# A three-block transformer kernel on eight cores: one weight pass over four PSUM banks in the expert layers, routing weights applied after the down projection, and full-width value matmuls

## What is computed

```python
def ffn(x, ...):                          # called twice
    x = x + mla(rmsnorm(x, w_ln1), ...)
    return x + moe(rmsnorm(x, w_ln2), ...)

def mla(xn, ...):                         # 16 heads of 64
    ...
    scores = einsum('bqhd,bkhd->bhqk', qq, kk) / 8      # causal
    probs = softmax(scores)
    y = einsum('bhqk,bkhd->bqhd', probs, v)
    return y @ W_o

def moe(xn, ...):                         # 7 routed experts, 2 per token
    shared = silu(xt @ Wg_s) * (xt @ Wu_s) @ Wd_s
    probs = sigmoid(xt @ W_router + routing_bias)
    scores, idx = top_k(probs, 2)
    wts = one_hot(idx, 7) weighted by scores / sum(scores)
    hmid = silu(xt @ Wg_r[e]) * (xt @ Wu_r[e])          # every e
    combined = sum_e wts[:, e] * (hmid[e] @ Wd_r[e])
    return shared + combined
```

## Time and profile before

| what | value |
|---|---|
| median of 2 runs | 8025.83 us |
| the two runs | 8085.91 and 7965.74 us |
| profiled execution, its time | 7965.88 us |
| its span, slowest core (core 7) | 7964.3 us |
| spans of the 8 cores | 7933.8 to 7964.3 us |
| mean granted clock of TensorE, by core | 0.780 to 0.786 of full speed |

### The profile page before, as it was taken

The page is one execution under the profiler, slowest core; times in us unless marked ns, Lnnn a source line. Parts: engine busy times, 40 slices in busy tenths (PEclk is TensorE's granted clock), DMA queues, the critical chain, the costliest instruction groups (busy, mean ns, idle before and its releaser), DMA issues.

```text
span 7964.3 us, 84976 instructions; the slowest of 8 cores (7933.8 to 7964.3 us)
## 1 busy us (share of the span) xinstructions
PE 5230.4 (66%) x21368; PEld 2042.4 (26%) x21368; DVE 2696.5 (34%) x5979; ACT 1441.0 (18%) x2520; POOL 110.8 (1%) x147
## 2 busy tenths in 40 slices
PE   2556544665642749999994853565662559999996
PEld 0222211111111314444442321111111223444442
DVE  2333335224223323333333354324223333333332
ACT  1222210442430101111111010342440001111110
POOL 0000000000000000000000000000000000000000
PEclk9556567777776879999997966677776779999998
DMA  5000132001014322222224123001003431221113
GB/s 118 6 6 14 17 83 52 8 11 22 11 25 96 78 43 32 32 33 32 32 32 96 21 42 88 10 11 22 11 8 68 102 64 22 39 36 32 32 32 85
DMA packets 390961, 319.60 MB, mean 40 GB/s; under 512 B 277889, under 2 KB 292737, under 8 KB 390530
## 3 DMA queue, kind: packets, MB, share of 16 engines
q0 software_dynamic: 73584, 145.83, 11.3%
q1 hardware_dynamic: 316946, 168.34, 8.7%
HBM read 287.70 MB, written 79.82 MB: 46 GB/s over the span
## 4 chain that ended last, share of the span: by engine, by line
PE 58%; DVE 12%; issue 9%; ACT 8%; DMA 7%; SPq 3%; DVEq 2%; ACTq 0%; POOL 0%; POOLq 0%
PE PS L210 57%; ACT SCF L220 6%; DVE SCF L215 3%; DVE SCB L215 3%; SPq L78 3%; DVE SM L215 2%; DVE XNT L215 2%; DMA d_xn<-SCF 1%; ACT SCA L220 1%; DMA SCB<-d_yraw 1%; DVE SCA L215 1%; DVEq L73 1%; PE PS L1169 1%; DMA d_lo<-SCB 1%; DVE STAT L215 1%
## 5 line engine op out<-in xcount | busy, mean ns | idle before, releaser
L210 PE MATMUL PS<-XNT,WB 128*128 128x512 bf16 x9472 | 2078.6, 383 | 560.7 <-DVE XNT L215 433.2
L210 PEld LDWEIGHTS PS<-XNT,WB 128*128 128x128 bf16 x9472 | 932.5, 99 | 1701.5 <-issue 605.1
L210 PE MATMUL PS<-WB,SCA 128*128 128x512 bf16 x4864 | 1094.1, 388 | 316.7 <-DMA SCA<-d_y 271.6
L220 ACT ACTIVATE SCF<-PS,SM 128x512 bf16<-128x512 f32 (+3 forms) x1280 | 771.0, 622 | 1093.1 <-PE PS L210 966.9
L210 PE MATMUL PS<-SCF,SCA 128*65 128x512 bf16 x1280 | 615.8, 481 | 421.1 <-DVE SCF L215 205.5
L220 ACT ACTIVATE SCA<-PS 128x512 bf16<-128x512 f32 x640 | 374.8, 595 | 2430.9 <-PE PS L210 2206.4
L210 PEld LDWEIGHTS PS<-WB,SCA 128*128 128x128 bf16 x4864 | 480.3, 100 | 920.6 <-issue 378.4
L215 DVE TENSOR_TENSOR R<-PS,R 128x512 f32<-128x512 f32 x640 | 442.7, 692 | 806.7 <-PE PS L210 806.7
L210 PE MATMUL PS<-XNT,SCA 128*128 128x512 bf16 x1280 | 614.4, 494 | 12.0 <-DVE SM L215 9.5
L215 DVE TENSOR_TENSOR SCF<-SCF,CONSTB 128x128 bf16<-128x128 bf16 x512 | 105.9, 207 | 964.9 <-ACT SCF L220 960.7
L210 PEld LDWEIGHTS PS<-SCF,SCA 128*65 128x65 bf16 x1280 | 150.6, 118 | 883.7 <-issue 860.2
(11 more groups left out here) (122 smaller groups left out, 2658.3 us busy)
## 6 DMA issues: line engine op xcount, KB each, us to landing
WB<-wg_r POOLq DMA_DIRECT2D x28, 1024.0 KB, 12.4
WB<-wu_r POOLq DMA_DIRECT2D x28, 1024.0 KB, 22.3
WB<-wd_r POOLq DMA_DIRECT2D x28, 1024.0 KB, 11.2
d_xn<-SCF SPq DMA_DIRECT2D x96, 256.0 KB, 2.1
sp_x<-R SPq DMA_DIRECT2D x8, 2048.0 KB, 17.3
R<-sp_x POOLq DMA_DIRECT2D x8, 2048.0 KB, 27.6
R<-x SPq DMA_DIRECT2D x4, 2048.0 KB
SCA<-XNT SPq DMA_DIRECT2D x32, 256.0 KB, 3.3
```

What stands on the lines that cost most here:

```text
L210: return e.matmul(out_ap, lhsT, rhs, start=start, stop=stop, tile_position=tp)
L220: return getattr(e, name)(*a, **kw)
```

## The change

Four things are done.

1. The value matmul of the causal attention takes 128 stationary columns from the same start, where it took 65, and writes all 128 rows of bank 5. Rows 65 on are not read. A memset clears the end of SCA once at the start.
2. Gate and up of a hidden tile `ic` take all 8 banks: banks 0 to 3 are gate for the four token blocks, banks 4 to 7 up. The loop over `c` is outside, the one over token blocks inside, so that 4 matmuls in a row have the same stationary operand.
3. The eviction follows in the same `ic`: silu of a gate bank (which then is free), then one VectorE multiply of the silu scratch with the up bank. `wts_prep` with its transposes, matmuls and copies is gone.
4. The down projection has `ic` outside and the two halves inside, and both banks are added behind the 16 matmuls. For a routed expert the addition is a `scalar_tensor_tensor` that multiplies by the token's weight from `WTS`, which is a column of one number per partition there.

```diff
+    v_op("memset", SCA[:, 16704:17408], 0.0)
...
-                            mm(PS[5][0:65, :],
-                               SCA[:, vcol(pkc) + 65 * hl:vcol(pkc) + 65 * hl + 65],
+                            mm(PS[5][:, :],
+                               SCA[:, vcol(pkc) + 65 * hl:vcol(pkc) + 65 * hl + 128],
                                SCF[:, 512 * pslot:512 * pslot + 512],
...
-                def wts_prep(ee):
...
-                wts_prep(0)
...
             for ic in range(ND):
-                for lh in range(2):
-                    t = 2 * ic + lh
-                    bks = (0, 1, 2, 3) if t % 2 == 0 else (4, 5, 6, 7)
...
+                for c in range(ND):
+                    for lb in range(4):
+                        bk = lb
+                        w0 = (p.use(f"ps{bk}") + [(s_tp, v_xnt), (s_dv, v_gain),
+                                                  (s_wl[0], vl_g)]
+                              if c == 0 else ())
+                        mm(PS[bk][:, :],
+                           WB0[:, c * D + 128 * ic: c * D + 128 * ic + 128],
+                           XNT[:, c * S + 512 * lb: c * S + 512 * lb + 512],
+                           start=(c == 0), stop=(c == ND - 1), wait=w0)
+                vm_g = s_mm.v
...
+                vm_u = s_mm.v
+                for lb in range(4):
+                    a_op("activation", out=SCA[:, 16384:16896],
+                         in_=PS[lb][:, :], func=AF.Silu,
+                         wait=[(s_mm, vm_g)] + p.use("silu_s"))
+                    va_si = s_ac.v
+                    p.release(f"ps{lb}", s_ac)
+                    v_op("tensor_tensor",
+                         SCA[:, 2048 * ic + 512 * lb:2048 * ic + 512 * lb + 512],
+                         SCA[:, 16384:16896], PS[4 + lb][:, :], ALU.mult,
+                         wait=[(s_mm, vm_u), (s_ac, va_si)] + p.use("silu_s"))
+                    p.drain("vector")
+                    p.release("silu_s", s_dv)
+                    p.release(f"ps{4 + lb}", s_dv)
...
-            if 0 <= e < ER - 1:
-                moe_state["wts_prep"](e + 1)
...
             for lc in range(NT):
-                for hf in range(2):
-                    bk = 2 * (lc % 2) + hf
...
+                bks = (0, 1) if lc % 2 == 0 else (2, 3)
+                for ic in range(ND):
+                    for hf in range(2):
+                        bk = bks[hf]
...
+                    if e >= 0:
+                        w0 = [(s_mm, vm)] + ([(s_dv, v_wts)]
+                                             if ei == 1 and lc == 0 else [])
+                        v_op("scalar_tensor_tensor", dst, PS[bk][:, :],
+                             WTS[:, 8 * lc + e:8 * lc + e + 1], dst,
+                             ALU.mult, ALU.add, wait=w0)
```

More of the change, by code:

```diff
@@ L1063, in phase_moe @@
         vmm0 = s_mm.v
-        bc_ready = {}
-        moe_state = {}
         v_op("memset", APx(PR, 7, [[128, 128], [8, 16], [1, 1]]), -1e30,
@@ L1160, in phase_moe @@
                 v_wts = s_dv.v
-                def wts_prep(ee):
[L1163 to L1177, removed]
-                    p.drain("vector")
[L1179 to L1184, removed]
-                        vm = s_mm.v
-                        dstb = (SCF[:, 512 * qb:512 * qb + 512] if par == 0 else
-                                SCB[:, 2048 + 512 * qb:2048 + 512 * qb + 512])
-                        v_op("tensor_copy", dstb, PS[7][:, :],
-                             wait=[(s_mm, vm)] + (p.use(f"bch{par}") if qb == 0 else []))
-                        p.release("ps7", s_dv)
-                    p.drain("vector")
-                    p.release(f"wrow{par}", s_dv)
-                    bc_ready[ee] = s_dv.v
@@ L1278, in phase_moe @@
-            for b_ in pbks:
-                p.release(f"ps{b_}", s_dv)
+            for ic in range(ND):
[10 more added lines that the diff above has]
+                vm_g = s_mm.v
+                for c in range(ND):
+                    for lb in range(4):
+                        bk = 4 + lb
+                        w0 = (p.use(f"ps{bk}") + [(s_tp, v_xnt), (s_dv, v_gain),
+                                                  (s_wl[1], vl_u)]
+                              if c == 0 else ())
+                        mm(PS[bk][:, :],
+                           WB1[:, c * D + 128 * ic: c * D + 128 * ic + 128],
+                           XNT[:, c * S + 512 * lb: c * S + 512 * lb + 512],
+                           start=(c == 0), stop=(c == ND - 1), wait=w0)
+                vm_u = s_mm.v
+                for lb in range(4):
+                    a_op("activation", out=SCA[:, 16384:16896],
[7 more added lines that the diff above has]
+                         wait=[(s_mm, vm_u), (s_ac, va_si)] + p.use("silu_s"))
+                    p.drain("vector")
+                    p.release("silu_s", s_dv)
+                    p.release(f"ps{4 + lb}", s_dv)
@@ L1280, in phase_moe @@
             v_hp = s_dv.v
-            if e >= 0:
-                p.release(f"bch{e % 2}", s_dv)
             p.release("wb0", s_mm)
             p.release("wb1", s_mm)
-            if 0 <= e < ER - 1:
-                moe_state["wts_prep"](e + 1)
             if ei < ER:
```

97 lines of the change are left out of this document (11 added, 86 removed).

## The result

| | before | after |
|---|---|---|
| median of the executions, us | 8137.83 (10, from 7965.74) | 8478.67 (11, from 8446.13) |
| profiled execution, us | 7965.88 | 8481.83 |
| its span, slowest core, us | 7964.3 (core 7) | 8480.3 (core 5) |
| the same core 7, us | 7964.3 | 8446.6 |
| after / before | | 1.061, 95% interval 1.0589 to 1.0631 |

The forecast was 8439 us and 5.9% more, the measured ratio is 6.1% more. The medians mix executions in which all cores hold their clock with others in which the cores of one die lose some of it for a while; the ratio compares only the former.

A forecast was written before the change was run, and what follows sets the result against it. The prediction took the expert layers to be bound by the columns TensorE streams. Its terms gave +241.6 us per call, +483 for two, less 10 for attention: +473 on 7965.88, so 8439 us, range 8310 to 8600.

The forecast's parts named there:

- rival 2, The clock falls further: Hidden-tile boundaries: two slow-clock stretches each, 3.4 us instead of 2.2, +134 us, 8573 us in all; chance 0.08.
- The pause: Boundary between hidden tiles: the fourth gate matmul waits for silu and multiply alternating on one scratch; 4.4 us lost, seven per expert.
- The clock: Behind each hidden-tile boundary: the clock falls to 1.2 GHz for a stretch, costing 2.2 us, scaled from 1.7 at 3.35.
- Before the down projection: End of gate and up: down starts 5.7 us behind the last up matmul against 3.5 before; +2.2 us per expert.
- After it: After the down projection: next expert's third and fourth gate matmul wait for both banks' additions; +1.3 us, six times a call.
- The weight row: Between gate/up and down: its transposes, matmuls and copies go, saving 20.0 us, six times a call, 120 us.
- The router: Before routed expert 0: first hidden tile's 64 matmuls run under the top-2, so the expert effectively starts 34.1 us earlier.
- Attention: Causal attention: 1280 value matmuls load faster at 128 columns; between 23 us won and 17 lost, taken as -10.
- The clock holds: Hidden-tile boundaries: three lone matmuls spread over the wait keep the clock up; 246 us less, 8193 us; chance 0.08.
- Not slower: Hidden-tile boundaries: the wait is short; break-even at 2.29 us each, 7924 us with 2.0 and no clock fall; chance 0.04.
- Reuse pays: Matmul stream: the same stationary operand four times in a row speeds matmuls up; 31 us less, 8408 us; chance 0.04.

The follow-up runs named there:

- filling the pause: Changed kernel plus fifteen repeats of the first gate matmul, five ahead of each of the second to fourth; ratio 1.038 to the kernel before.
- the two scratches: Changed kernel with two silu scratches used in turn instead of one; ratio 1.012 to the kernel before.
- taking half of it away: Changed kernel with the down loops as before, half outside, each bank evicted once done; 8449.34 us profiled, no ratio.
- the kernel without the row: Kernel before with the routing weight applied in the down projection's addition and wts_prep left out; 7685.43 us profiled, no ratio.
- where nothing stops: Kernel before with down-projection weighting and 128-column value matmul, plus first eight down token tiles waiting only for token blocks 0 and 1; fastest 7569.78 us, no ratio.

## Where the prediction held and where it failed, term by term

The mechanism, the sign and the size of the difference came out: +5.9% forecast, +6.1% measured. The terms gave 483 us for the expert layers and -10 for attention, 473 in all; the rows show 245.4 + 242.6 = 488.0 and -10.6, so 477.

What failed is the number that the sum starts from, and with it the upper end of the range. I added the terms to 7965.88 us, one profiled execution. It is as short as the shortest of what are now ten executions before (7965.74), whose median is 8137.83, 172 us more. Against that median a ratio of 1.061 makes 8634 us, and that is above my 8600, although the profiled execution of the changed kernel (8481.83) lies inside the range. The upper end held only what the terms could cost (rival 2, the lower clock), and nothing for how far the executions of this kernel lie apart, although the two times on the table already stood 120 us apart. A forecast from the trace should be read as a ratio.

Inside the sum no term failed by much, but two were mis-sized, and it is luck that they cancel: over 112 boundaries the pause was put 34 us too low and the fall of the clock 28 us too high.

- **The pause: 4.7 us, not 4.4.** The chain is the one described, silu and multiply in turn on one scratch. I had made two hand-overs too short. A multiply starts 0.17 behind a silu (3315.82 to 3315.99), not 0.11, which came from operations of one column in the router. The fourth matmul starts 0.46 behind the ScalarE result (3318.92 to 3319.38), not 0.25. So a product takes 1.55 us, and the fourth matmul comes at 5.35 instead of 5.03.
- **The clock: 1.95 us, not 2.2.** That it falls at each boundary was right, shown by filling the pause. The scaling with the length of the pause was wrong, shown by the two scratches. With the pause's error it comes to 6.65 against 6.6 per boundary.
- **Before the down projection: +2.5, not +2.2** (5.84 us of idle time against 3.35). The same hand-over of 0.17 instead of 0.11 comes in three times, and the first down matmul starts 0.25 behind the last multiply (3357.24 + 0.69 to 3358.18, core 7), where I had 0.12.
- **After it: +1.6 in the trace, not +1.3.** The addition that also multiplies takes 747 ns. How much of this wait arrives in the total stays open, since taking half of it away changed nothing.
- **The weight row: 20.4, not 20.0.** The rest is in the down projection behind it: 57.2 to 58.0 us for its 256 matmuls in the first call of the kernel before, 57.1 in the kernel without the row, and 55.4 where nothing stops.
- **The router: -5.7 forecast and -6.2 measured** for the stretch from the shared expert to routed expert 0. The fourth matmul of tile 1 starts 46.9 us behind the last transpose (2944.3 to 2991.20), 45.8 by my steps.
- **Attention: -10.6 measured, -10 forecast.** Here I had guessed a point between -23 and +17, so the exact hit is luck. The +17 took the width for the reason why the score matmuls show 494 ns and the value matmuls 481; a value matmul of 128 columns shows 487 ns in the changed kernel and one of 65 shows 496 (core 7 in both), so the width costs nothing there.
- **The rivals.** The clock holds: wrong, but the kernel with the filled pause shows what it would be, 8266.77 us at the fastest. The clock falls further: wrong, one stretch per boundary. Not slower: the break-even of 2.29 us per boundary stands against 6.65; the kernel with two scratches, at 6.65 - 3.4 = 3.2, is 1.2% slower, where that line gives 112 x 0.9 = 100 us or 1.3%. Reuse pays: wrong, 0.2157 against 0.2158 us.

So a large gain (154 and 148 us in the two calls for the weight row and the router, 5 for attention) was bought with a larger loss (56 boundaries of 6.65, 372 us a call, and some 30 us of longer waits around the down projections). The pause was not in the arithmetic of any engine; no engine has more instructions in the changed kernel.

## What to carry to other kernels

For each bank, count the matmuls that TensorE can still do between the end of the stage that fills the banks and the first matmul that wants this bank again. A loop order that touches four banks in four matmuls needs all four evicted at once, and one shared scratch then puts the whole eviction in series. Before a loop order is chosen for reuse of the stationary operand, look whether the weight loads are hidden: at 512 columns they are in this kernel, and there was nothing to gain.
